# Token routing moved from a phase of its own into the attention loop, batch by batch

## The reference, cut to what matters

```python
x = x + _L0_attn_ref(_layernorm(x), ...)     # 16 heads of 16, rotary mix of q and k, causal softmax
x = x + _L0_ffn_ref(_layernorm(x), ...)      # y = layernorm(x); logits = y @ gate_w  (8 experts)
    top_w, top_idx = jax.lax.top_k(logits, 2)
    top_w = jax.nn.softmax(top_w)
    ...                                      # gelu(y @ w1[e]) @ w2[e], weighted sum of the two
x = x + _L1_attn_ref(_layernorm(x), ...)     # cosine attention and an MLP
x = x + _L1_ffn_ref(_layernorm(x), ...)      # 64 experts, top 8, and 2 shared
```

## Time and profile before

| | us |
|---|---|
| median of 3 runs | 2749.5 |
| lowest, highest | 2744.93, 2750.41 |
| the profiled execution | 2746.9 |
| its span, first to last instruction | 2745.2 |

### The profile page before, as it was taken

How to read it: one execution, slowest core, us unless ns; L and a number is a source line. 1 busy time by engine, 2 the same in 40 slices (tenths; PEclk the granted TensorE clock), 3 DMA queues, 4 the chain that set the end, 5 groups by cost and what they waited for, 6 DMA issues and landing times. The chain is left out here.

```text
span 2745.2 us, 53741 instructions
## 1 busy us (share of the span) xinstructions
PE 2419.3 (88%) x20524; PEld 2156.7 (79%) x20524; DVE 1799.5 (66%) x3223; ACT 1342.6 (49%) x2061; POOL 824.5 (30%) x1226
## 2 busy tenths in 40 slices
PE   4999999953599999935788898789999999999999
PEld 3666666632599999924677787689999999999999
DVE  7666666664488888849998888267444454544544
ACT  1555555631377777633444453344454554545454
POOL 4555566317200000055677766410000000000000
PEclk7899999976799999967899999989999999999999
DMA  9995000003477677747656565144222222222222
GB/s 302 332 334 169 2 2 2 2 6 126 156 241 238 234 230 240 220 131 181 154 148 156 152 168 147 40 138 143 91 90 86 83 89 88 86 89 87 89 78 87
DMA packets 195374, 373.31 MB, mean 136 GB/s; under 512 B 28964, under 2 KB 105960, under 8 KB 194152
## 3 DMA queue, kind: packets, MB, share of 16 engines
q1 hardware_dynamic: 185816, 343.31, 40.7%
q0 software_dynamic: 9360, 27.27, 3.0%
HBM read 336.95 MB, written 100.66 MB: 159 GB/s over the span
## 5 line engine op out<-in xcount | busy, mean ns | idle before, releaser
L2314 DVE TENSOR_TENSOR e_h_lo<-e_h,e_h_hi 128x512 fp32r<-128x512 f32 x320 | 222.0, 694 | 300.2 <-ACT e_h_hi L2390 300.2
L2452 PE MATMUL e_h_ps<-e_yT_hi,e_w_hi 128*128 128x256 f32 x1280 | 362.9, 283 | 3.0 <-ACT e_h L2376 2.2
L2468 PE MATMUL e_y_ps<-e_w_hi,e_h_hi 128*128 128x256 f32 x1280 | 359.1, 281 | 2.4 <-DVE e_h_lo L2314 2.3
L2452 PE MATMUL e_h_ps<-e_yT_hi,e_w_lo 128*128 128x256 f32 x1280 | 358.7, 280 | 0.0
L2452 PE MATMUL e_h_ps<-e_yT_lo,e_w_hi 128*128 128x256 f32 x1280 | 358.7, 280 | 0.0
L2468 PE MATMUL e_y_ps<-e_w_lo,e_h_hi 128*128 128x256 f32 x1280 | 355.7, 278 | 0.0
L2468 PE MATMUL e_y_ps<-e_w_hi,e_h_lo 128*128 128x256 f32 x1280 | 355.7, 278 | 0.0
L2390 ACT ACTIVATE e_h_hi<-e_h 128x512 fp32r<-128x512 f32 x320 | 202.2, 632 | 276.7 <-DVE e_h L2309 220.5
L2376 ACT ACTIVATE e_h<-e_h_ps,e_b 128x512 f32<-128x512 f32 x320 | 218.9, 684 | 175.0 <-PE e_h_ps L2452 151.3
L2309 DVE TENSOR_TENSOR e_h<-e_h,e_spread 128x512 f32<-128x512 f32 x256 | 176.8, 691 | 133.5 <-ACT e_h L2376 132.4
L462 DVE TENSOR_REDUCE a_top<-a_ring 128x2 f32<-128x1024 f32 (+3 forms) x256 | 204.2, 819 | 72.2 <-PE a_ring L651 70.8
(11 more groups left out here) (371 smaller groups left out, 6772.6 us busy)
## 6 DMA issues: line engine op xcount, KB each, us to landing
e_w<-in_w SPq DMA_DIRECT2D x78, 1024.0 KB, 5.6
e_spread<-share_store SPq DMA_DIRECT2D x512, 128.0 KB, 2.8
a_keys<-rows_store SPq DMA_DIRECT2D x128, 256.0 KB, 5.0
a_queries<-rows_store SPq DMA_DIRECT2D x86, 256.0 KB, 4.9
a_running_hidden<-rows_store SPq DMA_DIRECT2D x42, 256.0 KB, 4.7
e_xs<-sorted_x SPq DMA_DIRECT2D x39, 256.0 KB, 5.1
sorted_y<-e_ys POOLq DMA_DIRECT2D x39, 256.0 KB, 5.9
e_stage_buf<-in_w_all SPq DMA_DIRECT2D x10, 512.0 KB, 3.9
```

Of the source, the lines that this page charges most:

```text
L2314: dve.tensor_tensor(h_parts[q % 2][1][:, :], h[:, q % 2, :], h_parts[q % 2][0][:, :], ALU.subtract).then_inc(h_lo.sem, h_lo.tick())
L2452: last = pe.matmul(h_ps[q % 2][:, cols], l, r, start=(m == 0), stop=(m == len(ops) - 1))
L2468: last = pe.matmul(y_ps[n][:, 0:D], h_parts[q % 2][a][:, n * P:(n + 1) * P], w2[b][:, c, :], start=(q == 0 and m == 0), stop=(q == CH - 1 ...
```

## The change

`route0_phase` is gone. Its work on a batch is put into `ORDER` one batch later, as new units in `BETWEEN`:

- `S0`, `S1`, `S2` (steps 3, 4, 4; DVE only): statistics, their aggregate and the seed, Newton rounds, now on DVE and of three instructions each instead of four on POOL.
- `N` (step 5, DVE): normalise into `y`, which is the storage of tiles 2 and 3 of `qk`.
- `U` (step 6): eight transposes on PE, high parts on ACT, low parts on DVE, into the `xnT` tiles. `L` (step 6): six matmuls that give logits by expert with the gate as the stationary side; ACT copies them out. `T` (step 6): turned to tokens by PE, copied by DVE.
- `C0` (step 6), `C1` (step 7; DVE): first and second pick. `K` (step 7): ranks on PE. `W` (step 7, DVE): rows.

`U`, `L`, `T` and `K` take places in the ring, `K`'s is given back by DVE in `W`. POOL's indirect DMAs of a batch (`scatter`, 8 of them) stand behind the stacks and `add_bias` of a later batch. Before the projection of tile 2 of a later batch is written to `qk`, DVE waits until the DMAs that read `y` have landed. The `n` unit of most batches moves from step 7 to step 3.

The last batch is routed behind the loop, then the slots are mapped, the first weights loaded and split, all in the same block. `sem_clear` stands before the experts instead of before the routing.

`stack_tile` has 8 instructions instead of 13: both q and k in one, and two copies of a sum written by one instruction whose output is twice as wide. The zeros go to `sorted_x` first, from `sorted_y`, and then to `sorted_y` in 15 copies of 2 MB, each issued when the one before has landed. Three more small loads and six more small DVE instructions stand in `constants`.

Before, the next stack stood directly behind the additions of the bias. The diff, cut to its core:

```diff
-                   ("b1", 2): ("t",), ("b2", 2): ("y",), ("a2", 1): ("n",)}
+                   ("b1", 2): ("t",), ("b2", 2): ("y",), ("a2", 1): ("n",), ("a2", 5): ("n",),
+                   ("b1", 3): ("S0",), ("b0", 4): ("S1",), ("b1", 4): ("S2",), ("b1", 5): ("N",), ("b0", 6): ("U",),
+                   ("b1", 6): ("L",), ("v2", 5): ("T",), ("b2", 6): ("C0",), ("b0", 7): ("C1",), ("b1", 7): ("K",),
+                   ("o", 5): ("W",)}
...
-                    of = s_ - 1 if extra in ("t", "y") else s_ + 1
+                    of = s_ - 1 if extra[0] in "tySNULTCKW" else s_ + 1
+                    if extra == "n":
+                        of = (s_ + 1 if s_ < 2 else B) if r_ == 1 else (s_ + 2 if s_ else B)
...
+            for e in range(2):
+                engine.tensor_tensor(pairs_of(turned[:, :])[:, :, :, :, e], pairs_of(qk[:, n])[:, :, :, :, 1 - e],
+                                     mix[:, :, :, :, e].broadcast_to([P, 2, H0, DH0 // 2]), ALU.mult).then_inc(step.sem, step.tick())
             engine.wait_ge(step.sem, step.at(step.n, turn))
-            for at in (0, DH0):
-                engine.tensor_tensor(q_stack[m][:, n, :, at:at + DH0], straight[:, 0], turned[:, 0],
-                                     ALU.add).then_inc(step.sem, step.tick())
-            for at in (0, 2 * DH0):
-                engine.tensor_tensor(k_stack[m][:, n, :, at:at + DH0], straight[:, 1], turned[:, 1],
-                                     ALU.add).then_inc(step.sem, step.tick())
+            engine.tensor_tensor(qk[:, n], qk[:, n], rope[:, n].unsqueeze(2).broadcast_to([P, 2, H0, DH0]),
+                                 ALU.mult).then_inc(step.sem, step.tick())
...
+            for at in range(TOKENS, END, TOKENS // 2):
+                spread("sorted_y", at, min(TOKENS // 2, END - at), spread_zeros)
+                sp.wait_ge(spread_zeros.sem, spread_zeros.at(spread_zeros.n))
+            sp.wait_ge(heads_out.sem, heads_out.at(PAIRS // 2, B - 2))
+            sp.dma_start(slot_ids, t["slot_ids"].rearrange("(o s) e -> o s e", o=1)).then_inc(slots_loaded.sem, slots_loaded.tick(16))
+            sp.wait_ge(mapped.sem, mapped.at(1))
+            e = sp.value_load(g.slot_expert[0:1, 0:1], min_val=0, max_val=E0 - 1)
+            sp.dma_start(g.w1[:, :, :], t["w1_0"][bass.ds(e, 1)].rearrange("o (c p) f -> p (o c) f",
+                                                                           p=P)).then_inc(first_w1.sem, first_w1.tick(16))
...
+            def scatter(q):
+                if q == 0:
+                    pool.wait_ge(zeros_spread.sem, ZERO_SPREADS * 16)
+                pool.wait_ge(rows_ready.sem, rows_ready.at(1, q))
...
                 if s == 1:
                     refine(2)
+                else:
+                    scatter(s - 2)
+            scatter(B - 2)
+            scatter(B - 1)
+            pool.wait_ge(written.sem, written.at(0, B))
...
+            def row_refine(q):
+                y_refined.n = 0
+                dve.wait_ge(y_step.sem, y_step.at(2 * TB + 5, q))
+                for i in range(3):
...
+            def normalise(q):
+                if q + 2 < B:
+                    dve.wait_ge(stacked.sem, stacked.at(2 * TB, q + 2))
+                if q:
+                    dve.wait_ge(written.sem, written.at(0, q))
...
+                    if r == 2 and s >= 3:
+                        dve.wait_ge(written.sem, written.at(0, s - 2))
                     biased(s, m, r, k)
...
+                if what == "T":
+                    pe.wait_ge(logits_taken.sem, logits_taken.at(1, s))
+                if what == "K":
+                    pe.wait_ge(rank_taken.sem, rank_taken.at(1, s))
...
             attention0_phase(nc, g, t)
-
             nc.gpsimd.sem_clear(g.spent)
...
-                    route0_phase(nc, g, t)
                 experts0_phase(nc, g, t)
```

669 lines of the change are left out of this document (317 added, 352 removed).

## The result

| | before | after |
|---|---|---|
| median, runs beside each other | 2749.4 (6 runs) | 2769.4 (6 runs) |
| lowest, highest | 2744.9, 2752.7 | 2762.6, 2775.0 |
| ratio after / before, 95% interval | | 1.0073, 1.0052 to 1.0094 |
| span of the profiled execution | 2745.2 | 2761.5 |
| first attention, to the last `add_proj` (T) | 580.4 | 678.3 |

The change makes the kernel 20 us slower; forecast were 16 to 18 us faster. The phase goes nearly as foreseen: 133.2 us become 43.9, the sum had 40. The loss is in the loop: T moves by 97.9 us where the sum had 75, and in the two profiled executions the experts and the second attention are 4 us longer each: 97.9 - 89.3 + 4.0 + 3.8 = 16.4, and the spans differ by 16.3. (Three of the six runs after took 2763 to 2766 us, three 2773 to 2775; the profiled one is of the first three.)

The account below looks back on a forecast made before the run. PE was taken to set the pace in attention, while routing left engines waiting for each other. Terms -93 + 22 + 32 + 18 + 4 - 1 = -18 us gave 2731 against a median of 2749.5; range 2698 to 2757, 8 in 10.

Parts of the forecast that it names:

- The phase, -93: Last `add_proj` to the experts' first transpose: 133.2 us become 40, with only the last batch's chain left there.
- PE's own work, +22: U, L, T and K inside the loop add 3.2 us to PE in each of seven batches.
- Order of DVE's units, +32: Steps 3 to 8: DVE's added work delays maxima, stalling PE 4.9 us in each of six batches, 3 in the last.
- The port, +18: Steps with POOL's stacks: S1 and S2 instructions wait for POOL, 3 us a batch in six batches; from 0 to 36.
- The zeros and the first copy, +4: First batch's indirect DMAs meet the zeros' copies, so one wait before a projection; from 0 to 20 us.
- (b): Sign: five steps, `b0` of step 3 to step 8, go from 30.4 to 41.5 us in batches 1 to 6.
- (c): Sign: PE waits for DVE's maxima at `b0` and for `a_both` or the ring at K; nearly nil before.
- (d): Sign: DVE's S1 and S2 rows take 0.5 to 1.3 us instead of 0.2 where POOL is busy.
- (e): Sign: DVE stands idle before the projection of tile 2 of batch 3 only.
- (f): Sign: DVE's new instructions take 11 us a batch.
- Rival 2: Loop: DVE becomes the bound through the lock in steps 4 and 5, 13 us or more a batch; 2765; chance 0.10.
- Rivals 1 and 3: 1: DVE not in the way, 2694, chance 0.15; 3: zeros hold the first scatter, 2757, chance 0.10 alone or in part.

Follow-up runs that it names:

- late_S: The changed kernel with `n` of all batches at step 7, S1 and S2 at step 5, N behind `b2` of step 5; 1.0006 of the kernel before.
- newton_pool: late_S with Newton's rounds on POOL between the stacks and the bias, and S2 gone from DVE; 1.0058 of the kernel before.
- spread2_noscatter: spread2 with the copies of rows to the DRAM table left out for batches 0 to 6; 0.9840 of the kernel before, T = 634.3.
- before_tiles: The kernel before with only the first experts' weight tiles laid out as in the changed kernel; experts' stage 477.6 us in one execution.
- before_stack_n3: The kernel before with `n` of batches 3 to 7 at step 3 and the new 8-instruction `stack_tile`; 1.0171 of the kernel before.
- before_n3: The kernel before with only `n` of batches 3 to 7 moved from step 7 to step 3; 1.0037 of the kernel before.
- spread2: The changed kernel with the routing chain spread up to step 8, S2 behind `a2` of step 5, S1's aggregates alone at step 4; 1.0026 of the kernel before.

## Why the prediction was wrong

Its own steps, and what the runs show in their place:

1. **The phase, -93: -89.3.** The chain was right to 1.4 us up to ACT's split. The term that failed is POOL's tail, 8.2 us from the last copy to the next block, which took 11.6. The clearing of semaphores is not it: from the landing of the last copy to DVE's first instruction of the experts it is 5.8 us in the kernel before, in late_S and in newton_pool alike. The landing is: the last copies now go out beside the weight loads. From `--dma` of late_S, 690 to 702 (median us to landing last):

```profile
sorted_x<-a_qk,rows POOLq DMA_INDIRECT x5, 5.9
```

   Before, the last ones landed after 2.4. The earlier trace rows held the 6.0 of copies beside weight loads, and I used it for the zeros alone. (The trace of the changed kernel does not tell its landings.)
2. **PE's own work, +22: right.** In spread2_noscatter a batch at full clock took 70.75 us, idle 3.85: 66.9 of work against 63.4 before (64.2 less 0.8), 3.5 a batch instead of 3.2.
3. **Order of DVE's units, +32 (4.9 a batch): half of that.** Without the stacks, idle rises from 0.8 to 3.2, 2.4 a batch. Where I placed it in step 7 it is there: 0.85 at K, 0.4 for the head update, 0.5 to 0.6 for the maxima behind W. Those of steps 3 to 6 exist only with the lock or where S2 stands ahead of `a2`.
4. **The port, +18 (3 a batch): 3.7 of idle time a batch, but elsewhere.** I counted the lock for S1 and S2, and put down the `n` unit at its own 1.4 us, moved to step 3 where the same paragraph says POOL is busy. It is what loses most: 2.9 of these 3.7 us are what `n` takes longer. Together, order and port were put at 7.9 us of stops a batch and made 6.1 (6.9 idle less 0.8 before), so stops are not what the sum lacked. I also took the shorter `stack_tile` for a gain (1 us a tile); a tile went from 9.07 to 8.6 us, and its 1.28 us instructions doubled what each locked instruction waits, 2.46 to 5.35 us for `n`. The rule that I quoted was the one for instructions with two SBUF inputs; the same section of the Trainium skill ("SBUF — State Buffer", "Who interferes with whom") says that `tensor_scalar` can take the shared pair too, and the rows of `n` agree (4.31 beside the stacks, 1.38 without).
5. **The clock: the failed step, put at nothing without a reason.** Lost clock in the five full batches is 1.5, 12.5, 11.7, 1.5 and 10.6 us, about 38. PE's busy time shows what of it counts: 365.8 us in the five stretches, where five times 66.9 are 334.5, so 31. The earlier trace rows held the price of a slow PE and I used it only for the end. The 78.7 us of these stretches are 17 of own work, 30 of stops and 31 of clock; forecast were 16, 39.5 and nothing. These 31 us carry the result over the 2757 of the range: without them it would be near 2738. The clock fell mostly behind the stops at `n`: without the stacks the five stretches are 34.6 us shorter, of which only 18 are idle time. So the lock's whole price is 7 us a batch where I had 3. That the stops were put too high and one error took back part of the other is luck. The undisturbed batches took 75.9 us, the forecast 75.3.
6. **The zeros and the first copy, +4: 0.** DVE never waited for a DMA before a projection.
7. **The start, -1: -0.9.** The first full batch begins its `x` at 69.3 and the next at 139.2, before 69.2 and 140.1.
8. **Later stages, 0: +7.7,** by one execution on each side; how much of it the change makes is not shown (see before_tiles). I had named over 2 us as what would refute the forecast, and held it impossible for lack of rows.

Of what was to show it: (b) the five steps took 42.3 us in a batch at full clock (410.93 to 453.19) and 46.9 in one with the low clock, forecast 41.5; (c) PE waits for maxima at `b0` and at K as said, for `a_both` only in the last stretch (1.2 us), and longest at `qk`, which I had not named; (d) and (e): the small rows are 0.58 to 0.66 us where POOL is busy, and no wait stands before tile 2; (f) DVE is busy 54.9 us in the batch from 381.48 and 42.2 in one before, 12.7 more, of which `n` takes 2.9 by the lock. Rival 2, "DVE becomes the bound and the gain is gone" by 13 us a batch, is the nearest: growth was 11.7 to 19 us a batch. It was given 0.10, with the right place (the lock in steps 4 and 5, one step late) and without the clock that makes it decide. Rivals 1 and 3 did not happen.

## What to carry to other kernels

When a step is moved on VectorE, price it at its new place: with the engine that shares its port at work there, and with the length of that engine's instructions, since each locked instruction waits for the rest of one of them. In a stage where PE is full at full clock, add to PE's waits what the granted clock takes behind them: beside 6.7 to 7.1 us of idle time a batch it took 1.5 to 12.5, and only experiments told how much. Removing one wait of an engine that is behind moves the next pieces into the place that it covered; take the cause away (here POOL's work) before moving units. And when an experiment misses, look at all engines at the place, not only at the one that sets the pace: here waits of ACT that nothing in the profile explains stood in ten of the kernels tried, and I had read their ratios by PE's and DVE's rows alone.

## What the runs showed of the hardware that was not expected

- The same 256-column instruction of VectorE took 0.34, 0.6, 1.1 or 1.3 us (four in 1.38, 2.46, 4.31 or 5.35) with POOL idle (the first), beside POOL instructions mostly of 0.5 to 0.8 us (the second), and beside those of 1.3 us.
- After one stop of 4.4 us the low clock lasted 7, 7, 3, 7 and 21 us in the five batches of before_stack_n3, with the same code. A stop of 1.5 us (before_n3) left it at full speed in all batches but one.
- Beside eight indirect DMAs of POOL, in some orders of the program and not in others, PE's issue slowed to one matmul in 0.7 us and ACT stood still up to 6.7 us at a time for an event that fits no instruction in the profile (14 to 32 us in 400); in spread2 without the DMAs both were gone.
- Indirect DMAs landed after 2.4 us alone and after 5.6 to 6.6 us beside loads of 1 MB (late_S, newton_pool).
- The phase that the change removes took 133.2 and 133.4 us in two executions and 141.2 and 141.3 in two others of kernels whose code there is the same, so 8 us of its price come and go; what with is open.
